# Row neighbours of a stencil by three SBUF transfers instead of six

## The reference

```
x = x + masked_softmax_pool(x)            # L0: scores from tanh(x W1 + b1) v, mask by the item's kind
x = x + layernorm_adapter(x)              # L1: relu(x W1[lang]) W2[lang], norm, gamma, beta by language
x = x + du_dt(x)                          # L2: the stencil, below
x = x + x @ W[cat] + b[cat]               # L3: one 512 x 512 matrix per category, 64 categories
```

```
yp_y  = jnp.pad(y, ((0, 0), (1, 1), (0, 0)), mode='reflect')
lap_y = yp_y[:, :-2, :] - 2.0 * y + yp_y[:, 2:, :]
du_dt = zX * lap_x + zY * lap_y + zR * y * (1.0 - y)
```

## Time and profile before

| | |
|---|---|
| time, median of 3 runs | 1086.45 us (1085.89 to 1087.23) |
| profiled execution: its own time | 1088.85 us |
| its span | 1087.1 us |
| PE busy | 1054.5 us (97%) |
| DVE busy | 960.1 us (88%) |
| POOL busy | 701.5 us (65%) |
| ACT busy | 510.6 us (47%) |
| granted clock of PE, mean | 0.998 of full speed |
| DMA | 268.87 MB, mean 247 GB/s |

### The profile page before, as it was taken

One profiled execution on the slowest core, in us unless ns is written; L12 is line 12 of the kernel. 1 busy time (PEld: TensorE's weight loads), 2 busy tenths in 40 slices (PEclk: granted clock), 3 DMA queues, 4 the chain that ended last, 5 costly groups with the idle time before them and its releaser, 6 DMA issues.

```text
span 1087.1 us, 22976 instructions
## 1 busy us (share of the span) xinstructions
PE 1054.5 (97%) x4912; PEld 658.7 (61%) x4912; DVE 960.1 (88%) x1962; ACT 510.6 (47%) x1422; POOL 701.5 (65%) x665
## 2 busy tenths in 40 slices
PE   5799999999999999999999999999999999999997
PEld 3566666666665566666666666666666666666652
DVE  5799998889989898998889998899999999989994
ACT  3444444444444444544545444445444444445441
POOL 3377667666666676666666766666766767667665
PEclk9999999999999999999999999999999999999999
DMA  8687897688878977776786868897878888887873
GB/s 332 214 258 224 254 309 239 199 266 263 250 224 292 299 248 230 232 238 189 239 263 198 267 204 269 265 281 236 262 240 269 252 260 256 284 269 215 265 227 116
DMA packets 134726, 268.87 MB, mean 247 GB/s; under 512 B 29138, under 2 KB 29156, under 8 KB 127172
## 3 DMA queue, kind: packets, MB, share of 16 engines
q1 hardware_dynamic: 97476, 199.83, 57.9%
q10 hardware_dynamic: 37120, 67.58, 20.4%
HBM read 243.21 MB, written 33.55 MB: 255 GB/s over the span
## 4 chain that ended last, share of the span: by engine, by line
PE 70%; issue 14%; POOL 8%; DVE 6%; DVEq 1%; ACT 0%; ACTq 0%; DMA 0%; POOLq 0%; SPq 0%
PE ps_out L431 30%; PE bank_hidden L385 8%; PE ps_adapt L413 8%; PE ps_attn L363 8%; PE ps_pool L404 7%; PE ps_x3T L421 4%; POOL b_wide L894 4%; POOL neighbours L875 2%; PE bank_hidden L397 2%; PE bank_scores L374 2%; DVE x L764 2%; DVE res L739 1%; POOL rstd L867 1%; PE bank_scores L391 1%; POOL above L887 1%
## 5 line engine op out<-in xcount | busy, mean ns | idle before, releaser
L431 PE MATMUL ps_out<-w3s,x3T 128*128 x1024 | 489.6, 601 | 2.3 <-ACT x3T L496 2.3
L431 PEld LDWEIGHTS ps_out<-w3s,x3T 128*128 128x128 f32 x1024 | 185.2, 191 | 189.8 <-issue 188.3
L887 POOL TENSOR_TENSOR above<-above,below 128x512 f32<-128x512 f32 x128 | 167.0, 1305 | 184.9 <-DMA above<-x 183.0
L764 DVE SCALAR_TENSOR_TENSOR x<-above,wide_rows,react 128x512 f32<-128x512 f32 x128 | 173.4, 1355 | 5.8 <-POOL above L887 5.1
L867 POOL TENSOR_TENSOR rstd<-var_eps,minus_half 128x1 f32<-128x1 f32 x128 | 70.1, 547 | 166.0 <-DVE var_eps L731 166.0
L881 POOL TENSOR_TENSOR react<-react,x 128x512 f32<-128x512 f32 x128 | 173.4, 1355 | 2.0 <-ACT react L539 2.0
L894 POOL TENSOR_TENSOR b_wide<-b_wide,x 128x512 f32<-128x512 f32 x128 | 165.6, 1293 | 1.4 <-DMA b_wide<-in_b 1.4
L875 POOL TENSOR_TENSOR neighbours<-x 128x510 f32<-128x510 f32 x128 | 132.6, 1036 | 11.4 <-DVE x L746 11.4
L517 ACT ACTIVATE square_junk<-ps_adapt,neg_mean 128x512 f32<-128x512 f32 x128 | 88.2, 689 | 110.0 <-DVE neg_mean L692 106.8
L385 PE MATMUL bank_hidden<-w_all,xts 128*128 x1024 | 138.8, 278 | 0.0
L385 PEld LDWEIGHTS bank_hidden<-w_all,xts 128*128 128x128 f32 x1024 | 124.2, 191 | 23.9 <-issue 20.6
(11 more groups left out here) (111 smaller groups left out, 1343.2 us busy)
## 6 DMA issues: line engine op xcount, KB each, us to landing
w3s<-in_w SPq DMA_DIRECT2D x128, 1024.0 KB
xts<-in_xT ACTq DMA_DIRECT2D x128, 256.0 KB, 4.6
xs<-in_x ACTq DMA_DIRECT2D x128, 256.0 KB, 5.0
b_wide<-in_b SPq DMA_DIRECT2D x128, 256.0 KB, 4.1
out_x<-res SPq DMA_DIRECT2D x128, 256.0 KB, 3.6
below<-x SPq DMA_DIRECT2D x128, 252.0 KB
above<-x SPq DMA_DIRECT2D x128, 252.0 KB
below<-x SPq DMA_DIRECT2D x256, 2.0 KB
```

What stands on the lines that cost most here:

```text
L431: mm = pe.matmul(ps_out[j.ring(2)][:, :], x3T[:, j.ring(2), k * P:(k + 1) * P], w3s[:, bass.ds(wslot * (K * D) + k * D, D)], start=(k == 0 ...
L764: nc.vector.scalar_tensor_tensor(x3[:, q, :], above[:, q, :], zy_t[:, bass.ds(i.n, 1)], react[:, q, :], ALU.mult, ALU.add).then_inc(x3_rea ...
L887: nc.gpsimd.tensor_tensor(above[:, q, :], above[:, q, :], below[:, q, :], ALU.add).then_inc(rows_ready, 1)
```

## The change

`above` and `below` become two halves of one tile `rows_near`. Both are filled in partitions 1 to 126 by one transfer each: `above[1..126]` from `x2[0..125]`, `below[1..126]` from `x2[2..127]`. What is left are partitions 0 and 127 of both halves. In partition 0 both hold row 1 (the mirrored one and the true one), in partition 127 both hold row 126. One transfer writes these four rows: its source is rows 1 and 126, each read twice. `SHIFTS`, the number of transfers that `sum_rows` waits for, goes from 6 to 3.

```
-        above = sb("above", [P, 2, D])
-        below = sb("below", [P, 2, D])
+        rows_near = sb("rows_near", [P, 2, 2, D])
+        above, below = rows_near[:, :, 0], rows_near[:, :, 1]
...
-        SHIFTS = 6
+        SHIFTS = 3
...
-                for to, at, rows, source in ((below, 0, P - 2, 1), (above, 2, P - 2, 1),
-                                             (below, P - 2, 1, P - 1), (below, P - 1, 1, P - 2),
-                                             (above, 0, 1, 1), (above, 1, 1, 0)):
-                    sp.dma_start(to[at:at + rows, q], x2[source:source + rows, q]).then_inc(shift_in[q], 16)
+                sp.dma_start(above[1:P - 1, q], x2[0:P - 2, q]).then_inc(shift_in[q], 16)
+                sp.dma_start(below[1:P - 1, q], x2[2:P, q]).then_inc(shift_in[q], 16)
+                sp.dma_start(rows_near[0:P:P - 1, q], x2[1:P - 1:P - 3, q:q + 1].broadcast_to([2, 2, D])
+                             ).then_inc(shift_in[q], 16)
```

## The result

The changed kernel is faster: 1083.42 us median of 20 runs (1077.20 to 1088.13) against 1087.47 us of the kernel before, measured beside it (20 runs, 1080.09 to 1096.40). The ratio is 0.996, 95% interval 0.9945 to 0.9976. A second measurement beside later experiments gave 1081.68 against 1087.68 us, 0.9932 (0.9909 to 0.9956). So the change is worth 0.4 to 0.7%, and I had forecast no visible difference with a lean to slower. All ratios are formed from the undisturbed executions of both kernels and are not the quotients of the two medians, which can differ from them by up to 0.13% (here 1081.68 / 1087.68 is 0.9945).

The account below looks back on a forecast made before the run. TensorE was taken as the bound, busy 997.07 of 1002.85 us in the steady stretch. Steady +3.0 and tail -0.9 gave +2.1, rounded down to +1.5 us on 1086.45: 1088.0 us, range 1082 to 1094.5.

Parts of the forecast that it names:

- SyncE's issues: SyncE's issuing of the shift transfers per item: 4.05 us falls to 2.24, worth nothing unless SyncE was late.
- The landing: Arrival of the shifted rows for L887: 0.9 us earlier taken, between 1.81 us earlier and 0.5 us later.
- More held L754: VectorE's L754 held by GpSimd's L887: 25 new collisions, 25 to 35 rows of 1.83 us where there were eight.
- this frees L764 in half of the cases: Of 13 new collisions with L764 held, the earlier previous L887 frees L764 in half, leaving about 6.5 costly.
- The price of the cheap ones: Slots behind a held L754 whose L764 was free: 0.13 us each, +2.4 us for 18.5 new ones.
- The price of the costly ones: Slots behind a held L754 whose L764 was held too: 0.90 us each, +5.9 us for about 6.5 new ones.
- Late landings: Two slots behind an L887 that waited long for rows cost 2.5 us together; earlier rows save about 1.6.
- The tail: Kernel's end hangs on the last L887, which waits 1.90 us for its rows: -0.9 us.
- rival 1: Steady stretch and tail: earlier rows free nearly all L764s, so every collision is cheap; 1080.2 us, chance 0.20.
- Rival 2: L754 against L887: L764 stays held as often as now, 0.90 us per case; +10.8, 1097 us, chance 0.22.
- Rivals 3 and 4: Rows' landing: unmoved, 1086.5 us, chance 0.10; or edge transfer up to 0.5 us later, 1089.5 us, chance 0.06.
- all the rest (small ones): Thirty-one small delays of steady slots, 4.3 us together in the kernel before, of which about 1 us goes.

Follow-up runs that it names:

- e2: Changed kernel with three single-row transfers that nothing waits for added behind each item's three: 1083.69 us, ratio 0.9971 to the kernel before.
- e8: Changed kernel with the small edge transfer issued ahead of the two large ones: 1090.26 us, ratio 1.0037 to the kernel before; measured again 1091.28 us, 1.0025.
- e3: Changed kernel with all transfers made, but L887 adds two constant halves and waits for no transfer: 1075.24 us, ratio 0.9883 to the kernel before.
- e6: Changed kernel with L887 also waiting for L754, and w3 loaded for the first two items only: 1076.09 us, ratio 0.9905 to the kernel before.
- e11: The changed kernel itself, unaltered, measured again with another profile: 1081.68 us, ratio 0.9932 to the kernel before.

## Why the prediction was wrong

The forecast was +1.5 us, lean to slower. It became -4.0 us, -6.0 the second time. Step by step:

- **SyncE's issues:** right. 2.38 us instead of 4.05, predicted 2.24, and no gain of SyncE's saved time is seen (e2).
- **The landing:** right. Measured from x2's end to L887's start in the cases where L887 waited for its rows, the median fell from 7.58 to 6.26 us where no w3 was loaded for the item before, and from 8.99 to 7.92 where one was. That is 1.3 and 1.1 us, against 0.9 taken. Its reason, that the large transfers decide, was right too (e8).
- **More held L754:** right. 32 rows in the first trace, 38 in the second, predicted 25 to 35. The kinds were right as well: ten (second trace: eleven) stood behind a held L764 and 20 (24) behind a free one, counted in the steady stretch, where the sum had 6.5 + 3.5 = 10 and 18.5 + 3.5 = 22. So "this frees L764 in half of the cases" came out.
- **The price of the cheap ones:** wrong, a failed step. It was "New cheap ones: 18.5 x 0.13 = +2.4", and 0.5 more for the old ones that become cheap. The 0.13 came from a slot in which L881 held L713 until 4.28 us into the slot, because its L887 had waited for its rows; no L754 was held before it (0.74 us at 96.23). In the changed kernel L713 behind such a held L754 ends 4.10 to 4.12 us in, in all 20 cases, and the slot stays at 8.04. The price is 0.00, and e3 shows it in 61 more slots.
- **The price of the costly ones:** wrong, and the larger error. The step was "New costly ones: 13 / 2, about 6.5 x 0.90", with the old ones at 0.93 as well: 5.9 + 6.5 - 3.2 = 9.2 us for ten. They cost 6.0 us for ten, 0.60 each, and in the second trace 6.5 for eleven, 0.59 each. The price is no constant. It follows L754's start, and seven of the ten started at 6.21 to 6.55 us into the slot, where the seven old ones had 6.72 to 7.28. I had priced by the start only in two classes, up to 6.3 and at 6.9 us, and hadn't moved the starts of the costly ones by the earlier rows.
- **Late landings:** wrong in the first trace. I had -1.6 us. Four slots of 3.4 us (two of them my 2.5 us) became five slots of 4.3 us; in the second trace three slots, 2.2 us. They hang on w3 (e6) and vary from run to run. One trace of before told me nothing firm of their cost.
- **The tail:** right in sign. The last L887 waits 1.38 us less, and the tail fell 1.84 us for 0.9 predicted.
- **Rivals:** rival 1 (earlier rows free nearly all L764) had the mechanism, though 32 and 34 L764 are still held. Its time of 1080.2 us is near the changed kernel's lower runs, and taken to its end (e3) it gives 1075.2. I gave it 0.20. Its price per slot, 0.07 to 0.13, was too high as well. Rival 2 wanted L764 held as often as before, and 79 became 32. Rivals 3 and 4 fell with the measured landing.

The rows of the kernel before ahead of the slot from which the 0.13 came (it starts at 98.10):

```profile
93.23 1.76 DVE L764 SCALAR_TENSOR_TENSOR x<-above,wide_rows,react 128x512 f32<-128x512 f32 x1
...
96.23 0.74 DVE L754 SCALAR_TENSOR_TENSOR react<-neighbours,wide_rows,react 128x512 f32<-128x512 f32 x1
...
97.53 1.27 POOL L887 TENSOR_TENSOR above<-above,below 128x512 f32<-128x512 f32 x1 [1.25 <-DMA above<-x]
```

The steady stretch, forecast and measured, as change against the trace of the kernel before in us:

| term | forecast | first trace | second trace (e11) |
|---|---|---|---|
| slots behind a held L754 | +5.6 | -0.5 | -0.1 |
| late landings | -1.6 | +0.9 | -1.2 |
| all the rest (small ones) | -1.0 | -2.2 | -2.6 |
| sum | +3.0 | -1.8 | -3.8 |

The collisions were to bring +5.6 us and brought next to nothing; that is the sign of the forecast. The gain of the stretch is in the small ones, which I had put at 1 us, and beside the stretch in the tail. Rounding +2.1 down and allowing for "the careful side" did not mend it.

What stays open. By theory A the time should follow the rows' arrival. With the edge transfer first, rows come 6.98 and 7.07 us behind x2 where no w3 was loaded for the item before, earlier than the 7.58 of the kernel before, and 9.13 and 8.89 where one was, against 8.99. L764 is held in 57 and 60 rows, fewer than 79. Yet it is 0.25 to 0.4% slower than the kernel before. Its traces have 16 and 18 slots over 0.25 us too long. Many of them stand behind an L887 that starts 2.1 to 3.0 us into its slot and holds no L754: there are 14 and 9 such starts in the steady stretch, against one in the kernel before and six and three in the changed one. So the median of the arrival doesn't tell the time, and its spread may be what counts; why such middling lateness is commoner there was not tested. Theory A is shown for the changed kernel and for e3, and it is incomplete for e8. Also not tested is how the time over what TensorE needs splits in an average run, since only single executions have traces.

## What to carry to other kernels

When two engines can hold each other, price a collision by what the next engine in line sees and not by how long the held row is: here 1.1 us were held each time, and TensorE lost nothing, or anything up to 1.1 us, by how far into the slot the held operation started. That in turn hung on whether the operation before had been held too. So look for the start up to which holding is free (here some 5.98 us into the slot) and ask what the change does to the starts. Such a kernel has no fixed schedule, so take the excess over the bound from several executions before working with its parts. Let the short operation that everybody waits for go first by a wait on purpose (one line gave 0.1 to 0.5%, by which measurement of the changed kernel it is set against), and issue the large transfers first when their data decide the arrival.

## What the runs showed of the hardware

- Operations of VectorE and GpSimd that start 0.01 to 0.02 us apart can settle either way. In the changed kernel L754 at 660.74 was held by L887 at 660.76. In e3, with the same 0.01 to 0.02 us between the starts, about half the slots went the other way and L887 took 1.85 us (503.79).
- An 8 KB transfer of 2 x 2 rows takes SyncE 0.71 us to issue, hardly less than one of 252 KB (0.80).
- Moving the same 8 KB transfer from third to first place made the rows 0.7 to 1.2 us later (medians) and the kernel 0.9% slower.
- Issuing a 1 MB load from the other queue leaves the total wait for the transfers beside it about as it was: 78.8 us, then 80.9 and 68.9 in two traces. The longest wait was 5.1 us, then 4.1 and 5.6.
- The granted clock differs between executions of one kernel (0.994 to 1.000 in the changed one). In the first trace a stretch of lower clock fell into the head, where one slot took 8.56 us at a mean share of 0.80 against 7.11 at 1.00.
